# Four graph layers on one core: the last hop in slots of two iterations with a turned product, and edge pairs turned in the banks of the walks

## The reference, cut to what matters

```python
x = x + L0(h)   # three weighted GCN convolutions, then a product
x = x + L1(h)   # GIN with edge features, two products with batch norms over all nodes
x = x + L2(h)   # x = x + relu((segment_sum(x[row], col) / deg) @ Wh.T + bh), 6 times
def L3(x):      # the last layer
    norm = dinv[src] * dinv[dst]
    h = tanh(segment_sum(norm[:, None] * (x @ W1)[src], dst) + b1)
    return h @ W2 + b2
```

## Time and profile before

| | us |
|---|---|
| three timed runs, median | 3483.99 |
| lowest, highest | 3480.55, 3488.85 |
| profiled execution | 3481.48 |
| its span, first to last instruction | 3479.7 |
| mean granted TensorE clock | 0.861 |
| PE, DVE, ACT, POOL busy | 75%, 64%, 58%, 41% of the span |

### The profile page before, as it was taken

How to read it: one execution, slowest core, us unless ns; L and a number is a source line. 1 busy time by engine, 2 the same in 40 slices (tenths; PEclk the granted TensorE clock), 3 DMA queues, 4 the chain that set the end, 5 groups by cost and what they waited for, 6 DMA issues and landing times. The chain is left out here.

```text
span 3479.7 us, 47724 instructions
## 1 busy us (share of the span) xinstructions
PE 2606.9 (75%) x11751; PEld 1653.7 (48%) x11751; DVE 2221.0 (64%) x8443; ACT 2032.0 (58%) x4419; POOL 1434.5 (41%) x1505
## 2 busy tenths in 40 slices
PE   5878767787677799999953448888888897757750
PEld 2555545555455544454422215565656565445530
DVE  6656777888977433333355338888888887775530
ACT  2778777767775455555555446666666665535520
POOL 6576764645535200000000006464656465344356
PEclk8999888989889899999965668899999997767775
DMA  4767454556656433434456445554545454322111
GB/s 99 204 194 210 144 155 137 175 162 184 196 180 178 133 137 135 137 134 134 137 170 203 151 154 163 156 156 145 168 143 161 142 163 131 98 79 71 48 35 41
DMA packets 526769, 499.35 MB, mean 144 GB/s; under 512 B 57504, under 2 KB 389541, under 8 KB 526410
## 3 DMA queue, kind: packets, MB, share of 16 engines
q1 hardware_dynamic: 475038, 409.93, 37.0%
q0 software_dynamic: 47184, 85.73, 9.6%
q10 hardware_dynamic: 4316, 1.13, 0.1%
HBM read 240.91 MB, written 260.14 MB: 144 GB/s over the span
## 5 line engine op out<-in xcount | busy, mean ns | idle before, releaser
L1748 POOL DMA_INDIRECT h_G<-step_tab,row_i x294 | 289.7, 985 | 543.9 <-DMA step_tab<-l_NR 301.8
L1748 POOL DMA_INDIRECT h_M<-step_tab,row_i x294 | 280.9, 955 | 196.3 <-PE h_P L1850 100.8
L791 PE MATMUL a_PA<-a_H,w 128*128 128x512 f32 x504 | 277.5, 681 | 96.3 <-ACT a_H L947 93.4
L1508 DVE TENSOR_SCALAR b_Y<-b_BP,col 128x512 f32<-128x512 f32 x148 | 111.1, 750 | 351.4 <-PE b_BP L1462 351.4
L220 ACT ACTIVATE l_ln_sd<-l_ln_mv,lneps 128x8 f32<-128x8 f32 (+1 forms) x136 | 40.9, 300 | 465.0 <-DVE l_ln_mv L2067 338.4
L1462 PE MATMUL b_BP<-b_Z,w 128*128 128x512 f32 x592 | 266.3, 592 | 0.0
L1490 ACT ACTIVATE b_Z<-b_BQ,bn 128x512 f32<-128x512 f32 x148 | 115.0, 777 | 257.1 <-PE b_BQ L1454 256.9
L2103 DVE TENSOR_TENSOR_SCAN h_T<-keep,h_T,h_P 128x512 f32<-128x512 bf16 x196 | 223.2, 1139 | 47.6 <-PE h_P L1850 34.8
L1550 POOL TENSOR_TENSOR b_d<-b_d,neghalf 128x1 f32<-128x1 f32 x1 | 0.6, 574 | 592.2 <-DVE b_d L1541 592.2
L1796 PE MATMUL l_XB<-ident,l_Y 128*128 128x128 f32 x592 | 103.1, 326 | 181.2 <-ACT l_O L1948 111.0
L282 POOL DMA_INDIRECT h_G<-msg_tab,row_i x147 | 144.2, 981 | 209.2 <-issue 110.7
(11 more groups left out here) (345 smaller groups left out, 6842.7 us busy)
## 6 DMA issues: line engine op xcount, KB each, us to landing
b_HI<-hin_tab SPq DMA_DIRECT2D x148, 256.0 KB, 2.8
y_tab<-b_Y SPq DMA_DIRECT2D x148, 256.0 KB, 2.0
l_Y<-y_tab SPq DMA_DIRECT2D x148, 256.0 KB, 3.7
l_X<-x_tab SPq DMA_DIRECT2D x148, 256.0 KB, 4.2
x_tab<-a_X SPq DMA_DIRECT2D x112, 256.0 KB
hin_tab<-a_HI SPq DMA_DIRECT2D x112, 256.0 KB
a_XR<-in_x SPq DMA_DIRECT2D x97, 256.0 KB, 4.3
out_rows<-l_O SPq DMA_DIRECT2D x97, 256.0 KB, 2.3
```

Of the source, the lines that this page charges most:

```text
L791: nc.tensor.matmul(PA[b][:, 0:nt * P], w[:, :], h[b][:, 0:nt, :].rearrange("p t d -> p (t d)"), start=True, stop=True).then_inc(done, 1)
L1748: pool.indirect_dma_start(out=GR_[i % 2][b][:, k, :], out_offset=None, in_=table[:, :], in_offset=bass.IndirectOffsetOnAxis(ap=row_i[:, t ...
```

## The change

It does three things.

1. In the last hop two iterations share a slot, seven slots in all, the first five with a pair. Tanh and the last product of an iteration move into the slot after (`end_prod(i - F0 - 2)` and so on), and two rounds of them stand behind the loop. The sums go through the product as the moving operand, with w31 held, so that features are on partitions: one matmul of 512 or 384 columns instead of one per tile. The factors come as a row, broadcast to all partitions from a new table in memory (`dinv_d`, written in the first phase, loaded per iteration into `DU`, 128 x 896 float32), and `end_scale` multiplies by it in one operation per half; the bias is given to tanh. `end_turn` and `end_copy` are gone. A second pair of buffers `l_Z` alternates with h_Z.
2. Edge pairs are turned into `PC` (even j) or `PH` (odd j) instead of `XB[j % 2]`, and wait for `x2(j-2)`; the wait for `norm2(j-2)` moves to `x3(j)`.
3. Constants of the first phase leave the memory that lives through all phases; `rb31` and `rb32` are not loaded. The first phase has one more add, root and reciprocal of 98x128 for the row of factors.

```diff
@@ first phase
+            nc.scalar.activation(ef["ef_zero"][:, :], ef["ef_one"][:, :], AF.Sqrt)
...
+            nc.vector.tensor_scalar(ef["ef_one"][:, :], ef["ef_cn"][:, :], 1.0, None, ALU.add)
...
+            nc.vector.reciprocal(ef["ef_one"][:, :], ef["ef_zero"][:, :]).then_inc(dinv_row, 1)
@@ slots
-    for i in range(IT):
-        slots.append(Slot3(left.popleft() if i % 2 and left else None, (STEPS * IT + i,)))
-    assert not left and slots[-1].pair is None and slots[-2].pair is None
+    for i in range(0, IT, 2):
+        slots.append(Slot3(left.popleft() if left else None, (STEPS * IT + i, STEPS * IT + i + 1)))
+    assert not left and slots[-1].pair is None
...
+    def turned_in(j, b):
+
+        return XB[j % 2][b] if is_d(j) else (PC, PH)[j % 2][b]
@@ SyncE, load_free(i)
+                elif F0 <= i < F0 + IT:
+                    t = first_tile(i % IT, 0)
+                    if i >= F0 + 2:
+                        sp.wait_ge(wk_z, 2 * (i - 2) + 2)
+                    sp.dma_start(DU[i % 2][:, :], dinv_d[0, t * P:(t + sum(SUB)) * P].partition_broadcast(P)).then_inc(du_in[i % 2], 16)
@@ TensorE, turn(j)
-                    if j >= 2:
-                        if is_d(j - 2):
-                            pe.wait_ge(o_set, 2 * (j - 2 - D0) + b + 1)
-                        elif full(j - 2, b):
-                            pe.wait_ge(normed2[b], no2(j - 2, b) + 1)
-                        else:
-                            pe.wait_ge(x2_set, q - 3)
+                    if is_d(j - 2):
+                        pe.wait_ge(o_set, 2 * (j - 2 - D0) + b + 1)
+                    elif is_d(j):
+                        pe.wait_ge(normed2[b], no2(j - 2, b) + 1)
+                    else:
+                        after(pe, x2_set, q - 3)
                     for k in range(4):
-                        last = nc.tensor.transpose(XB[j % 2][b][:, k * P:(k + 1) * P], Y[j % 2][b][:, k, :], ident[:, :])
+                        last = nc.tensor.transpose(turned_in(j, b)[:, k * P:(k + 1) * P], Y[j % 2][b][:, k, :], ident[:, :])
@@ TensorE, x3(j)
+                        if not is_d(j) and full(j - 2, b):
+                            pe.wait_ge(normed2[b], no2(j - 2, b) + 1)
@@ TensorE, hop_prod(i)
+                        last = nc.tensor.matmul(PH[b][:, 0:nt * P], w31[:, :], T[b][:, 0:nt * P], start=True, stop=True)
@@ TensorE, end_prod(i)
-                    pe.wait_ge(f_tt, n + 1)
+                    pe.wait_ge(f_th, n + 1)
+                    pe.wait_ge(*pc_user[b])
                     pc_user[b] = (f_o, n + 1)
...
-                        last = nc.tensor.matmul(PC[b][:, k * P:(k + 1) * P], Z[b][:, k, :], w32[:, :], start=False, stop=(k == nt - 1))
+                        last = nc.tensor.matmul(PC[b][:, k * P:(k + 1) * P], ZR[i % 2][b][:, k, :], w32[:, :], start=False, stop=(k == nt - 1))
@@ TensorE, order in a slot
-                for i in its[:1]:
-                    if i >= F0:
-                        end_turn(i - F0)
+                for i in its:
+                    if i >= F0 + 2:
+                        end_prod(i - F0 - 2)
                 for i in its[1:]:
                     hop_turn(i)
@@ ScalarE
+                    nc.scalar.activation(rows, rows, AF.Tanh, bias=col[:, C_B31:C_B31 + 1]).then_inc(f_th, 1)
@@ VectorE
+            def end_scale(i):
+
+                for b in range(2):
+                    n, t, nt = hop_at(i, b)
+                    at = b * SUB[0] * P
+                    dve.wait_ge(wk_prod, n + 1)
+                    dve.wait_ge(du_in[i % 2], 16 * ((i - F0) // 2 + 1))
+                    if i < F0 + 2:
+                        dve.wait_ge(wk_out, 2 * F0)
+                    else:
+                        dve.wait_ge(f_prod, n - 2 * F0 - 3)
+                    nc.vector.tensor_tensor(ZR[i % 2][b][:, 0:nt, :].rearrange("p t d -> p (t d)"), PH[b][:, 0:nt * P],
+                                            DU[i % 2][:, at:at + nt * P], ALU.mult).then_inc(wk_z, 1)
```

More of the change, by code:

```diff
@@ L1610, in build @@
     FR = [sb(ctx, f"l_FR{u}", [3 * (STEPS - 1), sum(SUB) * P], BF16) for u in range(2)]
+    DU = [sb(ctx, f"l_DU{u}", [P, sum(SUB) * P]) for u in range(2)]
+    ZR = [Z, [sb(ctx, f"l_Z{b}", [P, 4, D]) for b in range(2)]]
     ring = lambda n: [[sb(ctx, f"l_{n}{r}{b}", [P, 4, D]) for b in range(2)] for r in range(2)]
@@ L1714, in _ @@
                 j = sl.pair
+                if sl.its and sl.its[0] == F0:
+                    end_store(IT - 1)
                 if j is not None:
@@ L1781, in _ @@
         def _(pe):
-            pc_user = [None, None]
+            pc_user = [(x2_set, 2 * (D0 - 1 - (D0 - 1) % 2) + b + 1) for b in range(2)]
+            ph_user = [(x2_set, 2 * (D0 - 2 + (D0 - 1) % 2) + b + 1) for b in range(2)]
             def turn(j):
@@ L1907, in _ @@
                     x3(j)
-                for i in its[:1]:
-                    if i >= F0:
-                        end_prod(i - F0)
                 for i in its[1:]:
@@ L1913, in _ @@
                 late = j if j is not None and is_d(j) else None
+            for i in (IT - 2, IT - 1):
+                end_prod(i)
         @block.scalar
@@ L1985, in _ @@
                 j, its = sl.pair, sl.its
+                if its and its[0] == F0:
+                    pn.act_std(act, IT - 1)
+                    end_norm(IT - 1)
                 if late is not None:
@@ L2147, in _ @@
                 j, its = sl.pair, sl.its
-                for i in its:
-                    if i >= F0:
-                        if i == F0:
-                            end_rstd(IT - 1)
-                        else:
-                            end_rows(i - F0 - 1)
-                        messages(i)
+                last_hop = its and its[0] >= F0
+                if last_hop and its[0] == F0:
+                    end_rstd(IT - 1)
                 if j is not None:
@@ L2158, in _ @@
                         stats2(j - 1)
+                if last_hop:
+                    messages(its[0])
                 for i in its[:1]:
@@ L2167, in _ @@
                         end_rstd(i - LASTW - 1)
-                    for b in range(2):
-                        affine(i, b)
                     if i < F0:
+                        for b in range(2):
+                            affine(i, b)
                         update(i)
+                    else:
+                        end_scale(i)
                     if LASTW <= i < F0:
                         end_stats(i - LASTW)
+                if last_hop:
+                    if its[0] > F0:
+                        end_rows(its[0] - F0 - 2)
+                    messages(its[1])
                 if late is not None:
                     rows_out(late)
+                if last_hop and its[0] > F0:
+                    end_rows(its[1] - F0 - 2)
                 for i in its[1:]:
```

118 lines of the change are left out of this document (48 added, 70 removed).

## The result

| | before | after |
|---|---|---|
| timed runs, median (us) | 3483.80 | 3397.58 |
| lowest, highest | 3480.55, 3488.85 | 3395.74, 3398.60 |
| profiled execution | 3481.48 | 3398.49 |
| its span | 3479.7 | 3396.8 |
| mean granted TensorE clock | 0.861 | 0.860 |

The changed kernel takes 0.9745 of the time before, 95% interval 0.9733 to 0.9758. That is 86.2 us gained; the prediction was 3376 us, 21.6 us less than came out, inside its range of 3348 to 3417. In the profiled executions, on which the sum was made, 3398.5 stands against 3373.7: 24.8 us are to be found.

The account below looks back on a forecast made before the run. The end was taken as set by when the last hop's gathers start and how long its slots hold them. 3481.5 - 56.4 (edge pairs) - 52.7 (last hop) + 1.3 = 3373.7, plus 2.5 gives 3376 us; range 3348 to 3417.

Parts of the forecast that it names:

- Term 1, the release: Full edge pairs: turn released by the relu of y, x3 begins 1.69 us after the normalization instead of 7.10.
- Term 1, the size of x3: Full edge pairs: x3 keeps 6.69 us, so steps fall from 17.6 to 12.5 us, saving 56.4 us.
- The sign of term 1: Edge pairs: wrong if statistics wait for anything but x3 or the gathers start after 2040 us; 2026 expected.
- The signs of term 2: Last hop: wrong if slots exceed 32 us with VectorE waiting over 4 us before last rows, or scale waits for DMA.
- Term 2, the slot: Last hop: a slot of two iterations with a pair takes 28.6 us against 38.3; whole hop saves 52.7 us.
- m to scale(i): 6.9 us as now: Last hop's slot on VectorE: the scale follows the message sum by 6.9 us, unchanged from the kernel before.
- Term 2, the sixth slot: Last hop's slot without a pair, but the fifth pair's late half: TensorE reaches its second iteration's turn 16.3 us in.
- The broadcast of the factors: Last hop: 448 KB load per iteration expected covered 5 times or more; rival, slower than before, 2 in 100.
- The start: First phase: added reciprocal and three smaller operations of 98x128 cost 1.3 us on the path, bounds 0 and 1.3.
- TensorE stays fast: Rival for edge pairs and last hop: both x3 halves fast, slots of 27 us, 3350 us; 12 in 100.
- the slots shrank: Contradicts the last-hop rival that slots stay at 38.3 us, losing 39 us, total 3415; 13 in 100.
- the pairs left 17.6 us: Contradicts the rival that edge pairs stay at 17.6 us, bound by stores or landing loads, 3432; 8 in 100.

Follow-up runs that it names:

- e1_edges: Kernel before with only the edge-pair part (turn into other banks, wait moved to x3): 3440.81 us, 0.9875 of the kernel before.
- e2_hop: Changed kernel with the edge-pair part undone, the last hop's new slots kept: 3441.20 us, 0.9871 of the kernel before.
- 28 fillers: Changed kernel plus 28 small identity transposes per edge pair behind x3, on two slower chips: 3872.55 and 3854.50 us, 0.9645 and 0.9640 of the kernel before.
- e6_head: Changed kernel with the last product of i-2 and its rows at the slot's head, tanh a slot earlier: 3378.10 us, 0.9685 of the kernel before.
- e3_factors: Kernel before plus only the first phase's operations and store for the row of factors, which nothing reads: 3484.94 us, ratio 0.9995.
- e7_both: Changed kernel with 20 identity transposes per edge pair and the last product of i-2 at the slot's head: 3367.48 us, 0.9657 of the kernel before.
- 12 fillers: Changed kernel plus 12 identity transposes after each x3 of the full edge pairs: 3397.86 us, 0.9749 of the kernel before.
- 20 fillers: Changed kernel plus 20 identity transposes after each x3 of the full edge pairs: 3382.66 us, 0.9713 of the kernel before.
- e12_after: The changed kernel itself, run again on a slower chip: 3886.11 us, 0.9707 of the kernel before there.

## Why the prediction was right, and where it was off

- **The path.** Right. Scatters, last hop's slots, edge pairs before the first walk: everything between moved along unchanged (walks -1.1 us, scatters -0.4), and the two terms add up (e1_edges, e2_hop).
- **Term 1, the release.** Right: turn released by the relu of y, x3 1.69 us behind the normalization, 4.15 from statistics to normalization (4.14 taken), loads and stores covered (195 GB/s and queues 0.54 busy in the stage, 238 and 0.67 in the fast steps).
- **Term 1, the size of x3.** The term that was mis-sized. The prediction kept 6.69 us, one half slow and one fast as in the earlier trace rows; it is 7.76. The first half is as forecast (4.24 us), the second takes 3.52 where 2.44 was taken, so the step is 13.6 and not 12.5 (13.4 over the 11 steps). The clock fell where it was expected to hold: 0.64 after, 0.67 before, although the idle time ahead of the turn fell from 8.98 to 3.73 us. A shorter gap had been taken as worth at least as much clock as a long one. The place of x3 behind the start of the turn is nearly the same (first half 2.40 us before the change, 2.25 after; second half 6.65 and 6.49). What differs is when the clock rises: before, it was up when the second half began, in 10 of the 12 full pairs; after, in the pair shown, only at its last two products, 8.85 us behind the start of the turn. The first step after the change, with 3.60 us idle ahead of its turn, still had its second half fast and took the 12.4 us of the forecast:

```profile
1888.65 0.38 PE L1819 MATMUL l_XB<-split_r,ones 3*128 3x512 bf16 x1
```

  The next took 12.9, 13.3, 13.5 and 13.6 us. The fillers show that the clock is what x3 lacks; why it rises later behind a shorter gap stays open. The step given as its bound "both fast" (4.9, 10.7 us) is nearly what 28 fillers made (10.5).
- **The sign of term 1.** "Term 1 is wrong if [...] the gathers start after 2040": they start at 2042.0 us, where 2026 was forecast. So by its own sign the term failed, through the size of x3 (9.9 us) and the late start of the stage (5.4), and not through the release: in e1_edges, with the same steps and an earlier start, they begin at 2036.9. The signs of term 2 (slots over 32 us, a scale that waits for a DMA) did not come; VectorE does wait 7.2 us for TensorE, but before the scale.
- **Term 2, the slot.** Predicted 28.6 us each, measured 31.6, 28.6, 30.7 and (short, as the sixth slot has no x2; 25.0 forecast) 27.1. The step that failed is "m to scale(i): 6.9 us as now". The scale writes h_Z, and the last product of i-2 still reads it; `end_scale` waits for `f_prod`. The prediction listed this product as the next thing that VectorE waits for, but behind the scale, so that 1.6 us of scale lay in its shadow. They come after it: in the slot shown the product is out and the scale starts at 12.65 us (11.6 forecast for the product), the scale ends at 14.2, the rows at 15.3 where 13.2 was taken. That is the 2.1 us by which this slot is too long. In the three others the rows end at 14.7, 14.5 and 15.3 us, so that 7.0 of the 7.3 us arise ahead of this point. The slot of 28.6 us has the same wait (its scale starts at 11.84) and is as long as the forecast only by luck: 1.3 us too late at the rows, it wins 1.3 behind them with the high clock in its products. The slot of 31.6 us loses another 1.5 there, where its products take longer (2.08 and 1.65 us for the second last product, 1.16 and 0.94 in the slot of 28.6). e6_head removed the wait, and with it more than was missing.
- **Term 2, the sixth slot.** 20.2 us from its message sum (3230.87) to the gather that its second turn releases (3251.10), 16.3 forecast. The first gather to the first scatter is so made up: 34.1 for the first slot (34.0 forecast), the four next 118.0 (110.8), the sixth 20.2 (16.3), the last seven gathers 8.9 (8.8): 181.3 against 169.9. In the sixth slot TensorE's queue holds, between the pair's product and its rows, the product of the hop, which the forecast's list leaves out (2.4 us), and the second of the two last products waits 1.4 us; 3.8 of the 3.9 us. The row below names ScalarE for that wait, but the same wait stands in the slot shown above (1.44 us) with VectorE's rows as releaser, and here too the rows are being read out of the bank just then (from 3246.98), which points to the bank.

```profile
3235.13 3.62 PE L1837 MATMUL l_PC<-l_HT,w 128*128 128x512 f32 x4
3238.55 2.48 PE L1878 MATMUL h_P<-h_T,w 128*128 128x512 f32 x4
3240.95 0.38 PE L1844 MATMUL l_XB<-split_out,ones 3*128 3x512 bf16 x1
...
3247.80 0.37 PE L1887 MATMUL l_PC<-split_out,ones 3*128 3x512 bf16 x1 [1.43 <-ACT h_Z L1980]
...
3250.23 0.93 PE L1867 MATMUL h_P<-ident,h_M 128*128 128x128 f32 x7
```

- **The broadcast of the factors.** Right, and the rival falls: the loads of 448 KB landed 3.2 to 4.8 us after issue, no scale waited for one.

```profile
L1704 SPq DMA_DIRECT2D l_DU<-dinv_d x14: 319/326/488, 3050.5 to 3255.3; - x14
...
DMA to landing us min/median/max: 3.2/3.8/4.8
```

- **The start.** +6.7 us in the profiled execution, 1.3 forecast; by e3_factors the work itself costs nothing that can be told, and the rest is from execution to execution.
- **The rivals.** "TensorE stays fast" did not come true by itself (its 3350 is near what e7_both, 3367, and the 28 fillers aim at); the slots shrank; the pairs left 17.6 us. The sentence of the Trainium skill ("TensorE: Matmul & The Clock Gate", Part 1), "the default state is throttled, and activity releases the throttle", agrees with the fillers: the granted clock of the stage rose from 0.64 to 0.74 and 0.98. It does not tell the sign of the change itself, where the clock fell from 0.67 to 0.64 though TensorE was busy for 93.7 of 135 us and before for 74.3 of 150; and 12 fillers raised the mean and no settled step got shorter.

Of the 24.8 us: 9.9 are x3, 11.4 the last hop (7.3 its slots, 3.9 the sixth, 0.2 the rest), 5.4 the start of that one execution, less 1.7 of small differences.

## What to carry to other kernels

When a product moves a slot later, list for each buffer that it reads who writes it next: the write waits for the late reader, and everything that shares its engine waits with it. When a wait is shortened, do not take the clock of the operation behind it over from before, not even because TensorE idles less; size it from both levels, and look at the single operation, not at the mean clock of the stage. If TensorE idles between short bursts, a few products of a constant into a bank that will be overwritten anyway are a cheap test. Here 12 of them gave nothing and 28 gave 28 to 32 us.

## What the runs showed of the hardware

- The same repeated step can stay at either level of the clock. With 20 fillers, steps of 10.50 and of 13.6 us stand in one trace; with 28 nearly all are 10.5. After a first slower step (12.1 us) the trace with 20 has one of 10.7 and then settles at the long time (13.03, 13.34, 13.49, 13.58, 13.61 us); with 28, both steps of 12.1 us were followed by short ones again. The same row of step times (12.4, 12.9, 13.3, 13.5, 13.6) stands in the changed kernel on the first chip and on the slower one of e12_after.
- On two chips the kernel before took 4011 and 4001 us (medians) instead of 3484, at a granted clock of 0.80 to 0.82. In e12_after the edge stage ran at its usual pace (157.3 us). Against the changed kernel's first trace 358 us are lost ahead of that stage, some 110 in the walks, 14 in the last hop and 14 in the scatters. VectorE and ScalarE are seen to stand still together there, for instance for 9.2 and 9.1 us up to 321 us. In the waits of e12_after (who, for whom, us in total, times, longest):

```profile
DVE a_X L1184 <- remote: 164.7, 25, 22.0
ACT a_H L946 <- remote: 139.3, 17, 35.1
```

  Neither line has such a wait in the changed kernel's first trace. What it is that they wait for is not in the profile and stays open. The change took 0.9707 of the time there, with an interval (0.9658 to 0.9756) that holds the 0.9745 of the first chip.
